# A state-space layer on one core: plain drains of the projections, activations in one pass, one activation table, and a pair's inputs issued before the wait for its decays

## What is computed

```python
def selective_scan(u, dt, A, Bm, Cm, D):
    dA = jnp.exp(dt[..., None] * A)
    dBu = dt[..., None] * Bm[:, :, None, :] * u[..., None]
    _, h = jax.lax.associative_scan(comb, (dA, dBu), axis=1)      # h = dA * h_before + dBu
    return jnp.einsum('bldn,bln->bld', h, Cm) + u * D

def run(xz_, A_log_):
    xi, z = jnp.split(xz_, 2, axis=-1)
    xi = jax.nn.silu(causal_dwconv1d(xi.transpose(0, 2, 1), conv1d_w, conv1d_b)).transpose(0, 2, 1)
    x_dbl = xi @ x_proj_w.T
    dt = jax.nn.softplus(x_dbl[..., :DT_RANK] @ dt_proj_w.T + dt_proj_b)
    Bm = x_dbl[..., DT_RANK:DT_RANK + D_STATE]
    Cm = x_dbl[..., DT_RANK + D_STATE:]
    y = selective_scan(xi, dt, -jnp.exp(A_log_), Bm, Cm, D_ssm)
    return y * jax.nn.silu(z)

y = (run(xz, A_log) + flip(run(flip(xz), A_b_log))) @ out_proj_w.T
```

## Time and profile before

| What | Value |
|---|---|
| median of 3 runs | 19605.32 us |
| lowest and highest of the 3 | 19484.34 and 19623.32 us |
| the profiled execution's own time | 19497.92 us |
| its span, first to last instruction | 19496.2 us |
| TensorE busy, share of the span | 76% |
| VectorE | 73% |
| ScalarE | 66% |
| GpSimd | 49% |
| mean granted TensorE clock | 0.895 of full |

### The profile page before, as it was taken

How to read it: one execution, slowest core, us unless ns; L and a number is a source line. 1 busy time by engine, 2 the same in 40 slices (tenths; PEclk the granted TensorE clock), 3 DMA queues, 4 the chain that set the end, 5 groups by cost and what they waited for, 6 DMA issues and landing times. The chain is left out here.

```text
span 19496.2 us, 407673 instructions
## 1 busy us (share of the span) xinstructions
PE 14865.2 (76%) x155228; PEld 5461.5 (28%) x155228; DVE 14244.6 (73%) x12961; ACT 12924.9 (66%) x20898; POOL 9574.0 (49%) x8230
## 2 busy tenths in 40 slices
PE   5888888888885488888888888456666667568877
PEld 2333333333332222222222222111111111334444
DVE  8999999999993288888888888356666666356632
ACT  6999998989992377777777777256666666244423
POOL 5888877778781177777777777311111111000000
PEclk9999999999997788898898899788888889778888
DMA  2000000000005400000000000311111110531213
GB/s 78 12 12 12 12 12 12 11 12 12 12 12 144 103 17 17 18 17 18 17 18 17 17 18 16 94 28 31 31 31 31 31 31 23 168 71 33 35 44 128
DMA packets 773526, 710.83 MB, mean 36 GB/s; under 512 B 260272, under 2 KB 671056, under 8 KB 752984
## 3 DMA queue, kind: packets, MB, share of 16 engines
q1 hardware_dynamic: 691336, 584.14, 11.4%
q0 software_dynamic: 6720, 78.65, 1.7%
q10 hardware_dynamic: 74448, 33.14, 0.7%
HBM read 484.18 MB, written 211.60 MB: 36 GB/s over the span
## 5 line engine op out<-in xcount | busy, mean ns | idle before, releaser
L270 DVE TENSOR_TENSOR l_mx<-l_p_v,l_puN 128x2048 f32<-128x2048 f32 x2560 | 5634.5, 2293 | 127.6 <-PE l_p_s L485 115.2
L485 PE MATMUL l_p_s<-l_mx,l_w2z 128*32 128x512 f32 x32768 | 3817.1, 610 | 579.0 <-ACT l_mx L397 305.6
L290 POOL TENSOR_TENSOR l_mx<-l_pv,l_puP 128x2048 f32<-128x2048 f32 x1024 | 3715.8, 3645 | 315.2 <-PE l_p_s L485 309.8
L1270 POOL TENSOR_TENSOR l1m_hc<-l1m_hs,l1m_cs 128x512 f32<-128x512 f32 x2304 | 2927.5, 1271 | 8.5 <-DVE l1m_hs L1222 8.1
L1222 DVE TENSOR_TENSOR_SCAN l1m_hs<-l1m_da,l1m_carry,l1m_pu 128x512 f32<-128x512 f32 x2304 | 2824.5, 1268 | 105.8 <-ACT l1m_da L1140 2.2
L416 ACT ACTIVATE l_mx<-l_pv,l_puP 128x128 f32<-128x128 f32 x8192 | 2446.9, 393 | 0.8
L1212 DVE TENSOR_TENSOR l1m_pu<-l1m_pu,l1m_bs 128x512 f32<-128x512 f32 x2304 | 1478.3, 688 | 991.0 <-PE l1m_pu L975 991.0
L1896 ACT ACTIVATE l1d_clear<-l1d_pt 128x768 f32<-128x768 f32 (+2 forms) x1632 | 1261.0, 773 | 1298.9 <-PE l1d_pt L1641 1224.2
L1670 PE MATMUL l1d_ps<-l1d_part,l1d_xd 128*32 128x384 f32 (+2 forms) x13056 | 1399.6, 501 | 845.4 <-POOL l1d_xd L1961 377.5
L397 ACT ACTIVATE l_mx<-l_mx 128x2048 f32<-128x2048 f32 x1024 | 1954.4, 1909 | 54.1 <-POOL l_mx L290 53.6
L1140 ACT ACTIVATE l1m_da<-l1m_pr,l1m_an 128x512 f32<-128x512 f32 x2304 | 1457.5, 684 | 562.1 <-PE l1m_pr L968 394.9
(11 more groups left out here) (401 smaller groups left out, 21436.6 us busy)
## 6 DMA issues: line engine op xcount, KB each, us to landing
n_xt<-x_after SPq DMA_DIRECT2D x32, 2048.0 KB
l1m_sq<-seq SPq DMA_DIRECT2D x256, 144.0 KB
n_xt<-in_x_dram SPq DMA_DIRECT2D x16, 2048.0 KB
l_xs<-in_x_dram SPq DMA_DIRECT2D x128, 256.0 KB, 2.9
x_after<-l_ot SPq DMA_DIRECT2D x128, 256.0 KB, 2.4
x_after<-l1d_xh SPq DMA_DIRECT2D x32, 1024.0 KB, 5.2
x_after<-l_ot SPq DMA_DIRECT2D x64, 512.0 KB, 12.7
l3b_xs<-x_after SPq DMA_DIRECT2D x8, 4096.0 KB, 13.9
```

Source lines behind the costliest of these rows:

```text
L270: v.tensor_tensor(mx[:, r % QB, :, :, :], columns.unsqueeze(1).broadcast_to([P, 4, G, P]), rows.broadcast_to([P, 4, G, P]), ALU.max).then_ ...
L290: g.tensor_tensor(mx[:, r % QB, :, :, :], pv[:, u, :, :].unsqueeze(1).broadcast_to([P, 4, G, P]), rows.broadcast_to([P, 4, G, P]), ALU.add ...
L485: ins = pe.matmul(p_s[R * q:R * (q + 1), 512 * u:512 * (u + 1)], w2z[:, 31 - r:63 - r], mx[:, r % QB, q, :, :].rearrange("p t v -> p (t v) ...
L1270: g.tensor_tensor(hc[:, (3 * u + p) % 6, part, :], hs[:, p % 3, part, :], cs[:, u, :], ALU.mult).then_inc(hc_done, 1)
```

## The change

The order of the nine uses of `pp` becomes x0, x1, dt0, dt1, B, C, z0, z1, out: `x_proj` of half 1 moves from step 2 to step 1, the two `z_proj` from steps 1 and 2 to steps 7 and 8, and step 2 has none. ScalarE drains x and z as they are, x with its bias (`drain_x`, `Identity`) and z as a copy (`drain_z`, `Copy`), into a new tile `raw`. At step 2 one `Silu` over both halves makes `xi` of the next chunk (`gate_x`) and another makes `sz` of this chunk (`gate_z`), followed by an explicit load of the table `natural_log_exp_and_others`, which has `Exp` and `Ln`. New semaphores `xi_ready` and `sz_ready` tell TensorE and GpSimd of them; `dt_proj` waits for `xi_ready`. VectorE multiplies a pair's two inputs by B in one instruction of 1024 elements instead of two of 512. In `replicate` the wait for the decays (`wait_rates`) now stands behind the inputs.

```diff
-    X0, Z0, X1, Z1, DT0, DT1, BB, CC, OUT = range(USES)
+    X0, X1, DT0, DT1, BB, CC, Z0, Z1, OUT = range(USES)
...
             def dt_proj(n, un, ho):
+                pe.wait_ge(xi_ready, n + 1)
                 into_pp(n, (DT0, DT1)[ho])
...
                 if not (last and p + 1 >= PAIRS):
                     wait_inputs(ahead[0][0], ahead[0][2])
-                if not (last and p + 2 >= PAIRS):
-                    wait_rates(ahead[1][0], ahead[1][2])
                 for part in range(2):
                     if not (last and p + 1 >= PAIRS):
                         inputs_of(*ahead[0], part)
+                if not (last and p + 2 >= PAIRS):
+                    wait_rates(ahead[1][0], ahead[1][2])
                 for part in range(2):
                     if not (last and p + 2 >= PAIRS):
                         rates_of(*ahead[1], part)
...
                     if p == 1 and not last:
-                        z_proj(n, un, 0)
-                    if p == 2 and not last:
                         x_proj(n, un, 1)
-                        z_proj(n, un, 1)
...
+                        if p == 7:
+                            z_proj(n, un, 0)
+                        if p == 8:
+                            z_proj(n, un, 1)
...
+            def drain_x(n, hf, ahead):
                 act.wait_ge(pp_full, use_of(n, (X0, X1)[hf]) + 1)
                 if ahead:
-                    act.wait_ge(y1_done, n * 2 + (hf - 1))
-                act.activation(xi[:, un, hf, :], pp[:, :], ACT.Silu, bias=cols[:, 0, hf:hf + 1]).then_inc(pp_drained, 1)
-
-            def gate_z(n, un, hf, ahead):
+                    act.wait_ge(xi_ready, n)
+                act.activation(raw[:, 0, hf, :], pp[:, :], ACT.Identity, bias=cols[:, 0, hf:hf + 1]).then_inc(pp_drained, 1)
+
+            def drain_z(n, hf, ahead, uses=1):
                 act.wait_ge(pp_full, use_of(n, (Z0, Z1)[hf]) + 1)
                 if ahead:
-                    act.wait_ge(y2_done, n * 2 + hf)
-                act.activation(sz[:, un, hf, :], pp[:, :], ACT.Silu).then_inc(pp_drained, 1)
+                    act.wait_ge(sz_ready, n)
+                act.activation(raw[:, 1, hf, :], pp[:, :], ACT.Copy).then_inc(pp_drained, uses)
+
+            def gate_x(n, un, ahead):
+
+                act.wait_ge(pp_drained, use_of(n, X1) + 1)
+                if ahead:
+                    act.wait_ge(y1_done, n * 2)
+                act.activation(xi[:, un], raw[:, 0], ACT.Silu).then_inc(xi_ready, 1)
+
+            def gate_z(i, u):
+
+                act.wait_ge(pp_drained, use_of(i, Z1) + 1)
+                act.wait_ge(y2_done, i * 2 + 1)
+                act.activation(sz[:, u], raw[:, 1], ACT.Silu).then_inc(sz_ready, 1)
...
+                    if p == 2:
+                        if not last:
+                            a_of(n, un, jn)
+                            gate_x(n, un, True)
+                        gate_z(i, u)
+                        act.preload_act_table_set("natural_log_exp_and_others")
...
-                for part in range(2):
-                    bank = 2 * ((u + p) % 2) + part
-                    tile = pu[:, LC * bank:LC * (bank + 1)]
-                    dve.tensor_tensor(tile, tile, bs[:, u, :], ALU.mult).then_inc(dbu_done, 1)
+                bank = 2 * ((u + p) % 2)
+                tile = pu[:, LC * bank:LC * (bank + 2)].rearrange("p (a n) -> p a n", a=2)
+                dve.tensor_tensor(tile, tile, bs[:, u, :].unsqueeze(1).broadcast_to([NB, 2, LC]), ALU.mult).then_inc(dbu_done, 2)
...
             def gated(i, u, hf):
                 g.wait_ge(y1_done, i * 2 + (hf + 3))
+                if hf == 0:
+                    g.wait_ge(sz_ready, i + 1)
```

More of the change, by code:

```diff
@@ L843, in state_space @@
         sz = m.sb("sz", [P, 2, 2, LC])
+        raw = m.sb("raw", [P, 2, 2, LC])
         ex = m.sb("ex", [P, 2, LC])
@@ L936, in x_proj, with z_proj @@
                 ins.then_inc(pp_full, 1)
-            def z_proj(n, un, hf):
+            def z_proj(n, un, hf, uses=1):
                 into_pp(n, (Z0, Z1)[hf])
-                pe.matmul(pp[:, :], wz[:, hf, :], sq[:, un, 2, :], start=True, stop=True).then_inc(pp_full, 1)
+                pe.matmul(pp[:, :], wz[:, hf, :], sq[:, un, 2, :], start=True, stop=True).then_inc(pp_full, uses)
             def both_halves(out, w, n_in):
@@ L953, in b_proj, with c_proj @@
                 both_halves(pp[:, :], lambda hi: wb[:, hi, :], xi[:, un]).then_inc(pp_full, 1)
-            def c_proj(n, un, uses=1):
+            def c_proj(n, un):
                 into_pp(n, CC)
-                both_halves(pp[:, :], lambda hi: wc[:, hi, :], xi[:, un]).then_inc(pp_full, uses)
+                both_halves(pp[:, :], lambda hi: wc[:, hi, :], xi[:, un]).then_inc(pp_full, 1)
             def out_proj(i, use):
@@ L1028, in _ @@
             x_proj(0, 0, 0)
-            z_proj(0, 0, 0)
             x_proj(0, 0, 1)
-            z_proj(0, 0, 1)
             dt_proj(0, 0, 0)
@@ L1034, in _ @@
             b_proj(0, 0)
-            c_proj(0, 0, 2)
+            c_proj(0, 0)
+            z_proj(0, 0, 0)
+            z_proj(0, 0, 1, 2)
             wait_inputs(0, 0)
@@ L1092, in a_of @@
                 act.activation(an[:, un, :], ae[:, :], ACT.Copy, scale=-1.0).then_inc(a_ready, 1)
-            def gate_x(n, un, hf, ahead):
+            def drain_x(n, hf, ahead):
                 act.wait_ge(pp_full, use_of(n, (X0, X1)[hf]) + 1)
                 if ahead:
-                    act.wait_ge(y1_done, n * 2 + (hf - 1))
-                act.activation(xi[:, un, hf, :], pp[:, :], ACT.Silu, bias=cols[:, 0, hf:hf + 1]).then_inc(pp_drained, 1)
-            def gate_z(n, un, hf, ahead):
+                    act.wait_ge(xi_ready, n)
+                act.activation(raw[:, 0, hf, :], pp[:, :], ACT.Identity, bias=cols[:, 0, hf:hf + 1]).then_inc(pp_drained, 1)
+            def drain_z(n, hf, ahead, uses=1):
                 act.wait_ge(pp_full, use_of(n, (Z0, Z1)[hf]) + 1)
                 if ahead:
-                    act.wait_ge(y2_done, n * 2 + hf)
-                act.activation(sz[:, un, hf, :], pp[:, :], ACT.Silu).then_inc(pp_drained, 1)
+                    act.wait_ge(sz_ready, n)
[9 more added lines that the diff above has]
+                act.activation(sz[:, u], raw[:, 1], ACT.Silu).then_inc(sz_ready, 1)
             def softplus_parts(n, ho, ahead):
@@ L1121, in b_copy, with c_copy @@
                 act.activation(bs[:, un, :], pp[:, :], ACT.Copy).then_inc(pp_drained, 1)
-            def c_copy(n, un, ahead, uses=1):
+            def c_copy(n, un, ahead):
                 act.wait_ge(pp_full, use_of(n, CC) + 1)
@@ L1126, in c_copy @@
                     act.wait_ge(hc_done, n * D_IN + (6 - D_IN))
-                act.activation(cs[:, un, :], pp[:, :], ACT.Copy).then_inc(pp_drained, uses)
+                act.activation(cs[:, un, :], pp[:, :], ACT.Copy).then_inc(pp_drained, 1)
             def out_copy(j, u, use):
@@ L1144, in _ @@
             a_of(0, 0, 0)
-            gate_x(0, 0, 0, False)
-            gate_z(0, 0, 0, False)
-            gate_x(0, 0, 1, False)
-            gate_z(0, 0, 1, False)
+            drain_x(0, 0, False)
+            drain_x(0, 1, False)
+            gate_x(0, 0, False)
+            act.preload_act_table_set("natural_log_exp_and_others")
             softplus_parts(0, 0, False)
@@ L1152, in _ @@
             b_copy(0, 0)
-            c_copy(0, 0, False, 2)
+            c_copy(0, 0, False)
+            drain_z(0, 0, False)
+            drain_z(0, 1, False, 2)
             decays(0, 0, 0)
@@ L1163, in chunk @@
                         decays(n, un, p + 2 - PAIRS)
+                    if p == 2:
[3 more added lines that the diff above has]
+                        gate_z(i, u)
+                        act.preload_act_table_set("natural_log_exp_and_others")
                     if not last:
                         if p == 0:
-                            gate_x(n, un, 0, True)
+                            drain_x(n, 0, True)
                         if p == 1:
-                            gate_z(n, un, 0, True)
-                        if p == 2:
-                            a_of(n, un, jn)
-                            gate_x(n, un, 1, True)
-                            gate_z(n, un, 1, True)
+                            drain_x(n, 1, True)
                         if p == 3:
@@ L1181, in chunk @@
                             c_copy(n, un, True)
+                        if p == 7:
+                            drain_z(n, 0, True)
+                        if p == 8:
+                            drain_z(n, 1, True)
                     if p == 8:
```

4 lines of the change are left out of this document (2 added, 2 removed).

## The result

The changed kernel takes **18998.18 us**, the median of 4 runs (18992.7 to 19014.79), against 19552.94 us (19484.34 to 19623.32) for the kernel before on the same chip: a ratio of 0.9717, 95% interval 0.9674 to 0.9761. That is 555 us less where 280 less had been forecast. The 38 timings of the kernel before lie on two levels that differ in mean granted clock: 7 of them at 19484 to 19543 us, where the clock is 0.894 to 0.896, and 31 at 19598 to 19653 us, where it is 0.886 to 0.889 (for four of the 38 the clock is not on record). The changed kernel has one level.

What follows compares the result with a forecast made beforehand. Bound: TensorE's waits on ScalarE's silu and softplus chains, plus its half clock. Walk 38.6 + clock 1.9 = 40.5 us a chunk against 42.67, times 128: 280 us less, from 19550 to 19270 us; range 18980 to 19580.

Steps and rivals of the forecast that it cites:

- Both stalls: TensorE's waits of 2.09 us before z half 1 and 1.66 us for pair 7's decays; both were to go.
- One of the signs: What would show the forecast right, among other signs: output copies 40 to 41 us apart.
- the price of the half clock: TensorE's clock: 5.6 us a chunk at half clock, at 0.34 us each, adds 1.9 us.
- the full-clock rival: TensorE keeps 2.4 GHz with fewer waits: 38.6 us a chunk, 520 us less, 19030 us; chance 0.20.
- the half clock eats it: TensorE without slack: 8.5 us at half clock cost 0.5 each, 42.8 us a chunk, no change, 19560 us; chance 0.27.
- the walk: One chunk followed through TensorE and ScalarE at full clock, from step 2's replicate: 38.6 us, against 39.7 before.
- Rates apart at every step: Rates leave TensorE after the inputs at all other steps: 5.4 us a chunk, 410 us more, 19960 us; chance 0.07.
- The moved wait at nothing: In replicate: inputs go about 0.5 to 0.8 us ahead of the decays at steps 3 and 4; no gain counted.
- The merged multiplication at nothing: VectorE's one multiplication of 1024: from 0.1 us saved to 1.38 us taken; no gain counted.
- The table load: ScalarE: six loads fewer a chunk at 1.283 us, 7.7 us less; the skill's drain was not counted.

Runs made afterwards that it cites:

- e9: Kernel before with only the common Exp and Ln table loaded behind each Silu, 6 loads a chunk instead of 8: 19296.92 us, ratio 0.9838.
- e10: Changed kernel without the explicit table loads and with the wait for the decays back in front of the inputs: 19306.2 us, ratio 0.9842.
- e5: Changed kernel with two useless matmuls filling TensorE's wait at step 3 ahead of dt half 0: 18929.93 us, ratio 0.966.
- e12: e5 without the two explicit table loads, so 4 loads a chunk: 19172.3 us, ratio 0.9773.
- e1: Changed kernel with the wait for the decays moved back in front of the inputs: 19017.62 us, ratio 0.9697.
- e2: Kernel before with only the wait for the decays moved behind the inputs: 19506.03 us, ratio 0.9955.
- e8: Changed kernel with sums of pairs 0 to 2 moved to step 3 and of pairs 5 and 6 to step 8: 18730.09 us, ratio 0.9555.
- e4: Changed kernel with two multiplications of 512 by B in place of the one of 1024: 19005.06 us, ratio 0.969.
- e3: Changed kernel without the two explicit table loads, so 4 loads a chunk instead of 2: 19310.36 us, ratio 0.9844.

## Why the prediction was right or wrong

**The mechanism was right.** Both stalls went, TensorE sets the pace, dt half 0 waits for the silu (1.58 us; forecast 2.0), the softplus without loads lets the inputs of step 6 go at once, ScalarE is busy 24.9 us a chunk (25.1), VectorE's idle time before the multiplication is 4.1 us a chunk (below 6), and no load stands at the decays. `e9` and `e10` show both causes to be real and of about equal size. One of the signs did not come: the copies are 38.7 us apart and not 40 to 41.

**The step that failed: the price of the half clock.** The time lies in the stated range only because the range reaches down to the full-clock rival. The forecast itself was too small by half, and mostly by one term. The prediction took "two thirds of today's half-clock time, 5.6 us, at 0.34 us each: 1.9 us". The time at half clock was 4.5 us; the main error is the price. `e5` measured 0.11 us each (at most 0.14), 0.5 us a chunk in all, and `e12` 0.16. That is 1.4 of the 1.8 us a chunk by which the forecast (2.2 less) fell short of the measured 4.0. The 0.34 was itself an estimate from the kernel before, by comparing two chunks in another order, on the assumption that what stood behind the slow matmuls was on the path; I then carried it into a kernel where a wait stands behind them. What a slow stretch costs depends on what follows it, as step 4 of `e5` shows. The rival *the half clock eats it* made the same error with 0.5.

**The other 0.4 us: the walk.** 38.6 us at full clock, against 38.2 in `e5`. Set side by side, with 0 at the `replicate` of step 2: dt half 0 at 5.45 in the walk and 5.40 in the trace of after. The walk's ScalarE is then a little too slow: pair 5's decays end at 8.95, in `e5` at 8.80, and the two dt drains at 10.2, in `e5` at 9.96. dt half 1 waits for these drains, so it starts at 10.3 in the walk and at 10.01 in `e5`: 0.3 of the 0.4. The rates of step 4 wait 0.34 us in `e5` where the walk has 0.75, and in the changed kernel, at half clock, inputs and rates do not come apart there at all. The wait for the output was right, 28.0 - 27.1 = 0.9 us in the walk and 0.90 in the trace.

**The rival *full clock*** named the right time (19030) for the wrong reason: the clock was not full (0.94 in the stage), it just cost little. Full clock itself gives what `e5` has, 18930.

**Rates apart at every step** did not come: in the chunk above only steps 3 and 7 have inputs and rates apart, and step 7 had so before. **The moved wait at nothing** was right for this change (`e1`); in before the same line goes with the lower level (`e2`), and in `e8` it is probably worth 35 to 54 us. The forecast had no row for either. **The merged multiplication at nothing** was right in the time (`e4`); it takes 1.22 us, inside the bounds that were given (from 0.1 less than the two together to 1.38).

**The table load.** The Trainium skill, "ScalarE: Activation LUTs", section What ACT_TABLE_LOAD costs, adds a drain of about 1380 ns to the load at each switch to another set. Here the load starts 0.02 us after the preparation of A ends and the silu starts 1.29 us after the load does (9463.47 to 9464.76): no such drain is seen, and two loads fewer in the chain are worth 1.6 us a chunk (`e12` against `e5`), less than the 2.57 us of two bare loads.

**What stays open.** `e3`, `e9` and `e10` differ in order, loads and drains, and yet all three have chunks of 41.0 us with 6.8 us at half clock, within 14 us of each other in time. Chunk length and the falls of the clock may hold each other in place: with the falls filled (`e12`) the chunk of `e3` is 39.8. Why the three agree was not tested. For the same reason it is not settled how the two parts of the change add up, nor what the moved wait does in `e10` at a steady clock. Before was not run at full clock, so its 39.7 us a chunk stays an estimate, and with it the split of the 4.0 us into waits and clock. Its upper level has no trace; how it differs in the stage is open, beyond the lower mean clock.

## What to carry to other kernels

When a change takes a stall away, walk the new chain to the next wait and ask what owed work could stand there: moving sums into the two new waits brought 270 us on top of the change's 505 to 618, some 70 of them by way of the clock (`e5`), with only the order of TensorE's instructions changed and no work added or removed. Price a slow stretch of the clock by what is queued behind it, not by a figure from another order: where a wait followed, a us at half clock cost 0.11 to 0.16 us here. Look at all timings of the reference before naming a gain: nearly all of the 88 us of `e2`, and 80 to 110 of the 330 us of `e9`, are the distance between its two levels. And test a line that seems to do nothing again once the bound has moved: the moved wait did nothing in the changed kernel and seems to pay 0.2 us a chunk in `e8`.
